# A two-layer model on one core: cross attention 1 with keys a unit ahead, maxima rows from another queue, and scatters that may overlap within an expert

## The reference, cut to what matters

```python
x = x + tanh(g_xattn[0]) * L0_xattn(layernorm(x), ctx)      # cross attention 0
x = x + tanh(g_ffn[0])   * L0_ffn(layernorm(x))             # mixture 0
x = x + tanh(g_xattn[1]) * L1_xattn(layernorm(x), ctx, ctx) # cross attention 1
x = x + tanh(g_ffn[1])   * L1_ffn(layernorm(x))             # mixture 1

# cross attention 1: 16 query heads of 32, in 4 groups, each with one key/value head of 32
scores = einsum('bghsd,bgtd->bghst', qh, kh) / sqrt(32)
out = einsum('bghst,bgtd->bghsd', softmax(scores), vh) ; out @ Wc.T + bc

# mixture 0: 8 experts, 2 per token, inner size 192, shared part 1024
# mixture 1: 16 experts, 6 per token, inner size 352, shared part 704, with biases
probs = softmax(x @ gate.T); cw = weights of the chosen experts (0 elsewhere)
y = sum_e cw[:, e] * (silu(x @ W1[e].T) * (x @ W3[e].T)) @ W2[e].T  + shared(x)
```

## Time and profile before

| what | us |
| --- | --- |
| median of 3 runs | 2453.0 (2446.0 to 2457.29) |
| the profiled run, its own time | 2450.1 |
| span of the profile | 2448.2 |
| PE busy | 1968.5 (80%) |
| DVE busy | 1245.5 (51%) |
| POOL busy | 1015.5 (41%) |
| ACT busy | 815.7 (33%) |

### The profile page before, as it was taken

The page is one execution under the profiler, slowest core; times in us unless marked ns, Lnnn a source line. Parts: engine busy times, 40 slices in busy tenths (PEclk is TensorE's granted clock), DMA queues, the critical chain, the costliest instruction groups (busy, mean ns, idle before and its releaser), DMA issues. The chain is left out here.

```text
span 2448.2 us, 36252 instructions
## 1 busy us (share of the span) xinstructions
PE 1968.5 (80%) x10825; PEld 1599.1 (65%) x10825; DVE 1245.5 (51%) x2625; ACT 815.7 (33%) x1315; POOL 1015.5 (41%) x795
## 2 busy tenths in 40 slices
PE   4559989886782655878776887899999879999995
PEld 2247767765561443555444676779999778989995
DVE  7864553322221866788875566544444323434442
ACT  3451111132331454565674311113333222323331
POOL 5443644633343566675772110014342333433331
PEclk7779989998895677988988998999999889999998
DMA  8565846977756465221454000094649788474444
GB/s 296 167 241 181 257 126 227 288 229 224 178 116 145 120 152 159 40 36 34 110 149 153 21 29 26 1 338 85 156 80 286 227 280 239 84 224 80 80 80 107
DMA packets 130433, 370.56 MB, mean 151 GB/s; under 512 B 20456, under 2 KB 24424, under 8 KB 125080
## 3 DMA queue, kind: packets, MB, share of 16 engines
q1 hardware_dynamic: 83320, 264.33, 34.2%
q0 software_dynamic: 33600, 79.73, 17.5%
q10 hardware_dynamic: 13344, 24.32, 2.7%
HBM read 209.93 MB, written 149.74 MB: 147 GB/s over the span
## 5 line engine op out<-in xcount | busy, mean ns | idle before, releaser
L1582 PE MATMUL ps<-f_wb,f_xThi 128*128 x2088 | 541.7, 341 | 34.3 <-issue 24.6
L1698 POOL DMA_INDIRECT y_scratch<-f_yo,f_rows x150 | 238.2, 1588 | 495.1 <-ACT f_yo L1426 270.0
L1582 PEld LDWEIGHTS ps<-f_wb,f_xThi 128*128 128x128 f32 x2088 | 375.2, 194 | 63.1 <-issue 53.8
L1582 PE MATMUL ps<-f_wb,f_xTlo 128*128 x1044 | 348.7, 334 | 0.0
L1601 PE MATMUL ps<-f_wb,f_hThi 128*128 (+2 forms) x822 | 281.0, 423 | 16.1 <-DVE f_hTlo L1909 15.6
L728 POOL TENSOR_TENSOR a_elo<-a_e,a_ehi 128x768 f16<-128x768 f32 x128 | 217.4, 1704 | 159.4 <-ACT a_ehi L785 158.0
L1677 POOL DMA_INDIRECT f_xg<-xn_scratch,f_rows x150 | 159.2, 1061 | 217.8 <-PE ps L1566 161.5
L1927 DVE TENSOR_TENSOR f_g<-ps,f_bb 128x352 f32<-128x352 f32 x111 | 58.2, 524 | 342.2 <-PE ps L1582 263.7
L1426 ACT ACTIVATE f_yo<-ps,f_share 128x512 f32<-128x512 f32 x150 | 103.3, 689 | 299.1 <-PE ps L1601 186.4
L1582 PEld LDWEIGHTS ps<-f_wb,f_xTlo 128*128 128x128 f32 x1044 | 202.1, 194 | 0.0
L962 DVE TENSOR_REDUCE a_nmax<-ps 128x1 f32<-128x512 f32 x256 | 163.8, 679 | 48.7 <-PE ps L817 48.3
(11 more groups left out here) (241 smaller groups left out, 3897.6 us busy)
## 6 DMA issues: line engine op xcount, KB each, us to landing
f_wb<-w_scratch SPq DMA_DIRECT2D x16, 2816.0 KB
w_scratch<-f_stage_up SPq DMA_DIRECT2D x27, 1024.0 KB, 5.3
w_scratch<-a_stage_up SPq DMA_DIRECT2D x25, 1024.0 KB, 5.3
f_stage_raw<-in_f_w_dram SPq DMA_DIRECT2D x29, 768.0 KB, 7.4
f_wb<-w_scratch SPq DMA_DIRECT2D x16, 1024.0 KB
w_scratch<-f_stage_down SPq DMA_DIRECT2D x108, 128.0 KB
w_scratch<-a_stage_down SPq DMA_DIRECT2D x100, 128.0 KB, 2.3
f_wb<-w_scratch SPq DMA_DIRECT2D x8, 1536.0 KB
```

The source lines that it names most:

```text
L1582: mm = pe.matmul(out, xt[:, b % 2, k, :], weights(at, w, k, low), start=(m == 0), stop=(m == 3 * KD - 1))
L1698: pool.indirect_dma_start(y_d, bass.IndirectOffsetOnAxis(ap=rows_of[:, b:b + 1], axis=0), yo[:, b % 3, :], None, bounds_check=ROWS + P - 1 ...
```

## The change

It has three parts.

1. Mixtures, scatters: there are three semaphores `scattered[b % 3]`. POOL waits for scatter b - 1 and b - 2 with counts from the table (one less where that block has the same expert, so that the one in flight is not waited for), which it loads into registers. DVE computes these counts. ACT's wait is that for b - 3 as before. The spare rows are 3 x 128, so that pad blocks in flight together have rows of their own. SP waits at the end for the last three scatters.
2. Mixtures, prelude: `gwhi`, `brow` and `gwlo` are made after the first batch instead of before it.
3. Cross attention 1: keys are loaded three units ahead (their buffers are free by then) and behind the strips, the work on weight chunks comes behind both; the values are issued from ACT's queue at the start; the maxima rows are issued from ACT's queue after step 6; POOL's two memsets come after the first normalised x.

```diff
-        scattered = ctx.enter_context(nc.semaphore("scattered"))
+        scattered = [ctx.enter_context(nc.semaphore(f"scattered{i}")) for i in range(3)]
@@ cross attention 0, SP
-                    sp.dma_start(g["xn_d"][i][ROWS:ROWS + P, :], zero[:, 0:D + m["E"]]).then_inc(zero_out, 16)
-                    sp.dma_start(g["y_d"][i][ROWS:ROWS + P, :], zero[:, 0:D]).then_inc(zero_out, 16)
+                    for to, width in ((g["xn_d"][i], D + m["E"]), (g["y_d"][i], D)):
+                        sp.dma_start(to[ROWS:ROWS + SPARE, :].rearrange("(r p) d -> p r d", p=P),
+                                     zero[:, 0:width].rearrange("p (o d) -> p o d", o=1).to_broadcast([P, 3, width])
+                                     ).then_inc(zero_out, 16)
@@ cross attention 1, SP
                 load(0, 0)
                 load(1, 1)
-                for b in range(B):
-                    sp.dma_start(vraw[:, TB * b:TB * b + TB, :], ...).then_inc(v_in, 16)
+                strips(0, 0)
+                strips(1, 1)
+                load(2, 2)
                 sp.dma_start(wcT[:], ...)
                 sp.dma_start(bc[:], ...)
-                strips(0, 0)
-                strips(1, 1)
-                maxima(0, 0)
@@
                     if has_prepare:
-                        load(u + 2, (grp + 2) % GROUPS)
                         strips(u + 2, (grp + 2) % GROUPS)
-                    keep(u, 0)
-                    if has_maxima:
-                        maxima(u + 1, (grp + 1) % GROUPS)
-                    keep(u, 1)
+                        if not (isinstance(u, int) and u + 3 == UNITS):
+                            load(u + 3, (grp + 3) % GROUPS)
+                    if isinstance(u, int):
+                        if grp > 0:
+                            keep(u - 1, 1)
+                        keep(u, 0)
+                        if grp == GROUPS - 1:
+                            keep(u, 1)
@@ cross attention 1, POOL
+                pool.wait_ge(g["s_ln"], 2 * B + 1)
+                for u in range(2):
+                    prepare_pool(pool, u, u, 0)
+                pool.wait_ge(xc_ready, 2)
                 pool.memset(flt(ks[3 * HD:3 * HD + 2, :, :]), 1.0).then_inc(zero_set, 1)
                 pool.wait_ge(zero_set, 1)
                 pool.memset(v3[:, :, :, 3 * HD:3 * HD + 2], 1.0).then_inc(zero_set, 1)
@@ cross attention 1, ACT
+                for b in range(B):
+                    act.dma_start(vraw[:, TB * b:TB * b + TB, :], ...).then_inc(v_in, 16)
...
+                        if j == 6 and has_maxima:
+                            maxima_rows(act, u + 1, (grp + 1) % GROUPS)
@@ mixture
-            if b > 0:
-                eng.wait_ge(scattered, 16 * (EARLIER + b))
+            if b >= 0:
+                eng.wait_ge(scattered[b % 3], sums_of(b))
@@ mixture, ACT
-                act.copy(gwhi[:], gw[:]).then_inc(gwhi_ready, 1)
...
+                    if b == 0:
+                        act.wait_ge(par_in, PARAMS)
+                        act.copy(gwhi[:], gw[:]).then_inc(gwhi_ready, 1)
@@ mixture, POOL, scatter b
-                    added(pool, b)
+                    past = range(max(b - 2, 0), b)
+                    need = [sums_of(other) if EARLIER + other < 3 else
+                            pool.value_load(table[0:1, 1 + b - other, b:b + 1], min_val=16, max_val=sums_of(other))
+                            for other in past]
+                    for other, value in zip(past, need):
+                        pool.wait_ge(scattered[other % 3], value)
+                        pool.sem_inc(earlier_added, 1)
@@ mixture, DVE, tables
+                    link(dve.tensor_tensor(alike[0:1, 1:BLOCKS], ebf[0:1, 1:BLOCKS], ebf[0:1, 0:BLOCKS - 1],
+                                           ALU.is_equal))
+                    for back in range(1, 3):
+                        for r in range(3):
+                            last = dve.scalar_tensor_tensor(
+                                out=wants[0:1, back - 1, back + r:BLOCKS:3],
+                                in0=iota[0:1, 0:len(range(back + r, BLOCKS, 3))],
+                                scalar=float((EARLIER + 2 - r) // 3 + 1), in1=alike[0:1, back + r:BLOCKS:3],
+                                op0=ALU.add, op1=ALU.subtract)
...
+                    for back in range(1, 3):
+                        dve.tensor_scalar(table[0:1, 1 + back, back:BLOCKS], wants[0:1, back - 1, back:BLOCKS], 16.0,
+                                          None, ALU.mult)
```

More of the change, by code:

```diff
@@ L47 @@
 PAD_ROW = ROWS
+SPARE = 3 * P
 def flt(ap):
@@ L80, in build @@
         ps = ctx.enter_context(nc.psum_tensor("ps", [P, 8, 512], F32))
-        xn_d = [nc.dram_tensor(f"xn{i}_scratch", (ROWS + P, D + m["E"]), F32, kind="Internal").ap()
+        xn_d = [nc.dram_tensor(f"xn{i}_scratch", (ROWS + SPARE, D + m["E"]), F32, kind="Internal").ap()
                 for i, m in enumerate(MOE)]
-        y_d = [nc.dram_tensor(f"y{i}_scratch", (ROWS + P, D), F32, kind="Internal").ap() for i in range(2)]
+        y_d = [nc.dram_tensor(f"y{i}_scratch", (ROWS + SPARE, D), F32, kind="Internal").ap() for i in range(2)]
         bias_d = nc.dram_tensor("bias_scratch", (MOE[1]["E"], 2, MOE[1]["H"]), F32, kind="Internal").ap()
@@ L705, in _ @@
                 pool.wait_ge(zero_set, 2)
-                pool.wait_ge(g["s_ln"], 2 * B + 1)
-                for u in range(2):
-                    prepare_pool(pool, u, u, 0)
-                pool.wait_ge(xc_ready, 2)
                 keys_pool(pool, 0, 0)
@@ L753, in maxima_scalar, with maxima_rows @@
                 act.copy(mhi[:, grp % 2, :], ps[0:HPG * TB, MISC, 0:P]).then_inc(mhi_ready, 1)
+            def maxima_rows(act, u, grp):
+                act.wait_ge(mlo_ready, u + 1)
+                for i, m in enumerate((mhi, mlo)):
+                    act.dma_start(flt(qs[3 * HD + i:3 * HD + i + 1, HPG * grp:HPG * grp + HPG, :]),
+                                  flt(m[:, grp % 2, :])).then_inc(m_in[grp % 2], 16)
             def turn_scalar(act, b, k):
@@ L1091, in mixture @@
         share = sb(ctx, tag + "share", [P, BLOCKS])
-        table = sb(ctx, tag + "table", [1, 3, BLOCKS], I32)
+        table = sb(ctx, tag + "table", [1, 5 if BIASED else 4, BLOCKS], I32)
         first_of = sb(ctx, tag + "first_of", [1, E + 1], I32)
@@ L1135, in mixture @@
                 padv = sb(route, tag + "padv", [P, BLOCKS])
+                alike = sb(route, tag + "alike", [1, BLOCKS])
+                wants = sb(route, tag + "wants", [1, 2, BLOCKS])
             room = sb(early, tag + "room", [P, SIZE])
@@ L1304, in _ @@
                     stage.stored(sp, g["LAST"] - AT_ONCE)
-                added(sp, BLOCKS)
+                for b in range(BLOCKS - 3, BLOCKS):
+                    added(sp, b)
                 for t in range(B):
@@ L1488, in _ @@
                         mm.then_inc(xn_read, 1)
+                    if BIASED and b == 0:
+                        pe.wait_ge(bias_in, 16)
+                        pe.transpose(ps[0:2 * CHUNKS, XB, 0:P], b13[:].rearrange("p w c -> p (w c)"),
+                                     ident[:]).then_inc(brow_tr, 1)
                     if b > 0:
@@ L1730, in _ @@
                                           flt(xhi[:, k, S * b:S * b + S]), ALU.subtract).then_inc(lo_ready, 1)
+                    if b == 0:
+                        dve.wait_ge(gwhi_ready, 1)
+                        dve.tensor_tensor(gwlo[:], gw[:], flt(gwhi[:]), ALU.subtract).then_inc(gwlo_ready, 1)
                 for b in range(B):
@@ L1815, in tables @@
                     e, third, at, need, third_of = (
-                        tnum[0:1, 0, :], tnum[0:1, 1, :], table[0:1, 0, :], table[0:1, 1, :], table[0:1, 2, :])
+                        tnum[0:1, 0, :], tnum[0:1, 1, :], table[0:1, 0, :], table[0:1, 1, :],
+                        table[0:1, 4, :] if BIASED else tnum[0:1, 1, :])
                     link(dve.tensor_copy(e, ebf[0:1, :]))
@@ L1839, in rows @@
                     at = ps[:, XB, 0:BLOCKS]
-                    link(dve.tensor_scalar(red[:, 0:1], lane[:, 0:1], float(PAD_ROW + 1), None, ALU.add))
-                    link(dve.tensor_scalar(padv[:], at, 0.0, red[:, 0:1], ALU.is_equal, ALU.mult))
+                    for r in range(3):
+                        dve.tensor_scalar(red[:, r:r + 1], lane[:, 0:1], float(PAD_ROW + P * r + 1), None, ALU.add)
+                    link(dve.tensor_copy(padv[:, 0:1], lane[:, 0:1]))
+                    for r in range(3):
+                        last = dve.tensor_scalar(padv[:, r:BLOCKS:3], ps[:, XB, r:BLOCKS:3], 0.0, red[:, r:r + 1],
+                                                 ALU.is_equal, ALU.mult)
+                    link(last)
                     dve.scalar_tensor_tensor(out=rows_of[:], in0=at, scalar=-1.0, in1=padv[:], op0=ALU.add,
@@ L1923, in _ @@
                     if BIASED:
-                        buf = dve.value_load(table[0:1, 2, b:b + 1], min_val=0, max_val=2)
```

(1 more changed line is left out.)

37 lines of the change are left out of this document (15 added, 22 removed).

## The result

The median is 2376.1 us in 4 runs (2373.2 to 2383.2) against 2455.1 for the kernel before. The ratio is 0.9689 (95% interval 0.9656 to 0.9723), so the kernel is 3.1% faster, some 76 us. Predicted were 2364 and a gain of 89. In a second comparison of the same two kernels the ratio was 0.9692 (0.9656 to 0.9727).

A forecast was written before the change was run, and what follows sets the result against it. PE bounds mixture 1's routed part; mixture 0's routed part and cross attention 1 lose time to waits. Terms 0 - 4 + 1 - 40 - 30 - 5 + 1 - 12 = -89 gave 2364 us, range 2325 to 2415.

The forecast's parts named there:

- the three large terms: Scatters in mixture 0, -40 us; cross attention 1, -30; scatters in mixture 1, -12.
- the attention term: Cross attention 1: start -6.5, keys a unit ahead -48.5, late stage chunks +24, maxima rows +1; together -30 us, bounds -8 and -50.
- Scatters in mixture 0: Routed part of mixture 0: overlapping scatters win back 40 of about 47 us lost to weight fetches; bounds 20 and 47.
- Scatters in mixture 1: Routed part of mixture 1 and end: overlapping scatters give -12 us, limited by back to back fetches; bounds -25 and +5.
- The start of cross attention 1: Strips ahead of parameters, values from ACT's queue during the layer norm: -6.5 us, bounds -2 and -11.
- the one on the tables: Some ten more small DVE operations, partly on the path to the first gather: +1 us per layer, bounds 0 and 3.
- The preludes: Starts of mixtures 0 and 1: first normalise no longer behind the gate weights' cast, -4 and -5 us, bounds -1 and -9 each.
- Value loads on POOL: One or two register loads per scatter, two taking 1.0 to 2.4 us per block, hidden within an expert; +1 per layer's tail.
- The fourth rival: Routed parts: POOL becomes the bound through slow value loads, about 2736 us at 3 us per load; chance 0.06.
- That scatters gain nothing: Rival 1: scatters held by a fetch land together at its end; mixtures give 0 to -10, about 2412 us; chance 0.11.
- That the stall only moves: Rival 2, cross attention 1: late stage chunks cost 9.7 us in each of five units; attention -8, total 2386; chance 0.19.
- The rule weighed there: DMA queues share 16 engines, so other issuers save only issue time: at most 1.2 us per unit for the maxima rows' move.

The follow-up runs named there:

- experiment 2: Kernel before with the scatter part alone, but each scatter always waits for the two before it, so nothing overlaps, loads made but unused; ratio to before 1.0055.
- experiment 8: The kernel after run and profiled again, unchanged; median 2374.7 us, routed part of mixture 1 again 17.7 us shorter than before.
- Experiments 1 to 3: Kernel before with scatter, attention or prelude part alone: ratios 0.9826, 0.9882, 0.9969; scatters without overlap: 1.0055; kernel after with nine table operations made four times: 0.9738.
- experiment 4: The kernel after with every value load of POOL made twice, the first not used; ratio to the kernel before 0.973.
- experiment 7: Kernel after with maxima rows issued by SP again: ratio to before 0.9693; with chunk work first and SP issuing them only in the loop's units: 0.9685.

## Why the prediction was right, and where not

The time was inside the range and the signs of the three large terms were right. Of 89 us, 75 came in the profiles. That the attention term fits as well as it does is in part luck: its pieces missed by 3 to 4 us each, and not all the same way.

- Scatters in mixture 0 (-40): right, -36.5 and -32.1 together with the others, -42.9 alone, shown to be the overlap by experiment 2. I had not counted that PE's busy time, at the higher clock, falls by 9 us in it.
- Scatters in mixture 1 (-12, bounds -25 and +5): -17 to -18 or -8 to -11, in part by whether one scatter meets a fetch (experiment 8). The limit set by the back to back fetches is argued, not tried.
- Cross attention 1 (-30): the number is right, and the main step is the one named: keys' wait gone, a chunk's wait of 10.9 (7.5 said) in its place, a unit of 31.6 us. By the casts of the maxima the units with chunks gave 28.5 us in all, not 24.5, and unevenly: three of the first units 5 to 7 us each, but the very first none (36.6 against 36.4, with a chunk's wait of 9.8 in the place of that for keys). The loop's units lost 0.1 to 0.5 each, not 0.1: the wait for `mlo` is long (6.4, I had 2.8), but nearly all of it is covered.
- The start of cross attention 1 (-6.5) is a step that failed. The first cast of the maxima stands 46.9 us behind the read back, 49.2 before; but in three other kernels that have before's order it stands at 47.3 to 47.6, so the move gave 0.4 to 2.4 us. The strips were not held on SP's queue by the values: before, SP issued the first of them at 788.08, 0.6 us behind the start of ACT's cast of `qhi` (787.45). What was won lies behind the issue: from that of the `qlo` strip to PE's first raw scores it took 12.0 us before (9.9 to 10.4 in the three others) and 8.3 after. And 1.4 us of that went again, since the keys came later and `qhi` behind them. That both come from what else is in transfer at the time (values and `wcT` before the strips then, values beside the keys now) is argued from the order of the issues; no run moved the values alone.
- A step that failed in size is the one on the tables: "+1 us in each layer". I took ten small operations by 0.24 and said that a part lies on the path. Experiments 1 to 3 show 3 to 5 us in each layer: there were more (14 in all: 404 records on DVE became 418), none is covered, since the sums into x, on which PE's shared part waits, stand behind them on DVE, and more is lost than their own time. That is some 6 of the 14 us.
- The preludes (-4 and -5): -3.4 in mixture 1, and in mixture 0 nothing alone and some 3 us beside the scatter part. The idle of the earlier trace rows was the upper bound, and what came late next were the writes of the normalised rows, which the next batch needs out of its buffers.
- Value loads on POOL: 0.46 us each, at the low end of the bounds, and for the most part hidden. Beside the overlap, which I had, it is POOL's queue that hides them, since it makes them while POOL executes; experiment 4 hints that not all of it is hidden. The fourth rival, POOL as the bound, is refuted. That scatters gain nothing is refuted by experiment 2. That the stall only moves is half true: a wait of 10.0 us became one of 10.9 at another place, but 5 us of that unit stayed won, since PE and DVE work on in the new one (6.8 and 8.0 of 12 us). In the first of the units the rival was right.
- The rows of the maxima landed in 1.8 to 1.9 us from ACT's queue too (1.9 in the earlier trace rows), and experiment 7 found no gain in the move. The rule weighed there, from the Trainium skill, "Trainium Kernel Development and Optimization", Key Constraints, that several issuers save only issue time, agrees with that.

## What to carry to other kernels

Before you change a queue's order, write down what now stands behind the moved item and when it is wanted: the place of the next stall (here the chunk's, 10.9 us where 7.5 was worked out) can be read off the old trace. A wait that goes on an engine with slack is worth only what its followers lose by it. Small operations put on an engine for which the bound engine waits cost their full time, and here more. Small transfers that a big one holds up gain by being made independent of each other, and here two in flight gave most of it.

## What the runs showed that I had not expected

- Gathers and scatters that are not held up start 3.3 us apart for a pair (1821.84 and 1825.11 in after): that is POOL's own pace (1.59 and 1.06 us busy, 0.3 idle behind each), and it has room for two value loads.
- Whether the scatter behind one that is issued near a fetch can start 6 us later or only 11 to 14 hangs on less than a microsecond (fetch 1.6 or 2.2 us behind it).
- PE's matmuls in the routed part of mixture 0 took 197.2 us of busy time at a granted clock of 0.89 and 187.9 at 0.95: the idle time that went was 27 us, and the busy time fell by 9 with it.
